# Self attention scores of a decoder layer: products over 64 rows of the array at a time, or over all of it with zero-padded queries and a third key buffer

## The chip, the cores and the metric

One core of one Trainium2 chip runs the whole kernel. The metric is the device time of one execution in microseconds (us). Three executions of the kernel before took 706.29, 706.56 and 707.81 us, so the median is 706.56 us.

## What is computed

The reference is one decoder layer with three sub-layers, each behind a layer norm and added back to its input. `x` is 16 batches of 256 tokens of 128 numbers; the context has 1601 tokens per batch.

```python
xh = x.reshape(b, c, h, he).transpose(0, 2, 1, 3)            # 16 heads of 8
q, k, v = jnp.split(einsum('bhce,ef->bhcf', xh, Wqkv) + bqkv, 3, axis=-1)
att = einsum('bhqe,bhke->bhqk', q, k) / sqrt(8)
att = softmax(att * tril(ones((c, c)), k=-1))                # masked scores count as 0
x = x + (einsum('bhqk,bhke->bhqe', att, v)) @ Wr + br
x = x + cross_attention(layernorm(x), ctx)                   # 1601 keys
x = x + routed_mlp(layernorm(x), top 2 of 8) + shared_mlp(layernorm(x))
```

The change touches only the two products of queries with keys in the self attention.

## The kernel before, in words

**Batches in a pipeline.** Each engine's stream is written out by hand: a `begin()`, a `step(i)` for each batch in the middle, and a `finish()`. In step i the matmul engine (PE) works on the scores of batch i, on the second scores and values of batch i-1, on the output of i-2, on cross attention of i-3 and the gate of i-4. Engines meet by semaphores only, and every engine's list is in order: what waits holds up all behind it.

**Parts.** q and k are split into three bf16 parts each (`split_cast` on ACT, `split_rest` on POOL, L2139 and L2141), so that one bf16 product over 48 rows (6 pairs of parts by 8 elements of a head) has nearly fp32's accuracy. The 16 heads are in two halves, a = 0 and 1, of 8 heads. The tile `parts` goes to DRAM and comes back in another order: `write_parts(b, a)` issues four DMAs on SP's queue (L640 to `q_parts`, three times L642 to `k_stack`), and `load_stack(b, a)` waits until those four have landed, and then issues four loads: keys into `kst` (L655) and three times queries into `qst` (L658). Both tiles have two buffers, for even and odd batches.

**Two scores.** `scores(b, u)`, called for u = 0 to 11, makes two things of each head. For batch b it makes *alpha* (L800), scores with queries on the output's partitions, of which DVE takes the row maxima (L1748, L1752, semaphore `alpha_max`); a last matmul adds the mask (L808, L810). For batch b-1 it makes *gamma* (L803), scores with keys on the partitions and minus the maximum already in them: rows 48 to 50 of the stacks hold the maximum in three bf16 parts and ones. ACT takes the exponential (L1476, `p_exp`), POOL sets the masked part to zero (L2201), and `values` (L840, L843) multiplies by v, in four column strips of 32. Units with u % 3 = 0 hold four heads of 128x128, the others two of 128x256.

**The place in the array.** `rows_of(b, a) = 64 * ((a + b) % 2)`: a batch's half lies in partitions 0 to 47 or 64 to 111, and the half with the same a of the next batch lies in the other one. In a unit, alpha of b and gamma of b-1 therefore use different row halves of the array, and the code issues them in turn.

**Maxima.** At the end of a batch `maxima_T` (L827) transposes the maxima, ACT copies them to `mT` (L1449), and `write_maxima(b)` on SP's queue (L668, two DMAs, one for each half) puts them into rows 48 to 50 of `qst`. `scores(b + 1, 0)` waits for that (`mrows0_in`), for the stack (`stack0_in`), for `alpha_max` and for `p_exp`, all ahead of its first matmul.

**The order on SP's queue**, L640 to L668 among the loads of weights and context:

```python
load_w13(f)                # f = i + 1
write_parts(f, 0)
load_stack(f, 0)
write_maxima(i)
load_info(i - 2, 0), load_infoT(i - 1), load_info(i - 2, 1)     # 1.6 MB of context
write_parts(f, 1)
load_stack(f, 1)
```

Of the kernel before, what the change touches and what calls it, by code (L numbers as in the profile page):

```python
# [16 lines left out]
P = 128  # L17
# [39 lines left out]
QROWS = 48  # L57
KROWS = 51
# [7 lines left out]
def decoder_kernel(nc, x, ctx, ctxT, consts, wq, wk, wv, wr, wx, gate, w13, w2, out):  # L66
    with ExitStack() as stack:
# [3 lines left out]
        def sem(name):  # L71
# [44 lines left out]
        qst = [sb(f"qst{n}", [P, HG, S], BF16) for n in range(2)]  # L116
        kst = [sb(f"kst{n}", [P, HG, S], BF16) for n in range(2)]
# [35 lines left out]
            "split_cast", "split_sub", "parts0_out", "parts1_out", "stack0_in", "stack1_in",  # L153
# [17 lines left out]
        def rows_of(b, a):  # L171

            return 64 * ((a + b) % HA)
# [52 lines left out]
        for n in ("ln3_stats", "ln3_aggr", "ln3_eps", "ln3_rstd", "xn3_done", "xn3T_ps", "xn3T_sb", "x3_hi_done", "x3_lo_done",  # L226
                  "lg_ps", "lg_sb", "route", "shifted", "ex_done", "weigh", "picked", "rank_ps", "rank_read", "row_x", "placed", "sent",
                  "tri_done", "mx_zero", "pad_done", "home_done", "spare_out", "filled_set", "final", "slots_done", "blank_out", "pad_at_done", "info0_in", "info1_in", "x3_copied",
                  "up_ps", "silu_done", "h_done", "y_ps", "shared_done",
                  "in0", "in1", "in2", "in3", "in4", "in5", "sx_ps", "sx_hi", "sx_lo", "sup_ps", "sgate_done", "shid_done", "sT_ps", "sT_sb",  # L230
                  "sy_ps", "sy_sb", "sum_done"):
            s[n] = sem(n)
# [348 lines left out]
        def _(sp):  # L581
# [53 lines left out]
            def write_parts(b, a):  # L635

                if live(b):
                    sp.wait_ge(s["split_sub"], 2 * b + 2)
                    after(sp, f"stack{a}_in", 64 * b)
                    sp.dma_start(dq[a].rearrange("c p t -> p c t"), parts[64 * a:64 * a + 64, :, 0, :]).then_inc(s[f"parts{a}_out"], 16)  # L640
                    for c, (s0, s1) in enumerate(((0, 3), (3, 5), (5, 6))):
                        sp.dma_start(dk[a, s0:s1].rearrange("c p t -> p c t"),  # L642
                                     parts[64 * a:64 * a + 64, c, 1, :].unsqueeze(1).to_broadcast([64, s1 - s0, S])
                                     ).then_inc(s[f"parts{a}_out"], 16)

            def load_stack(b, a):

                if live(b):
                    sp.wait_ge(s[f"parts{a}_out"], 64 * b + 64)
                    if b < 2:  # L650
                        sp.wait_ge(s["pads_done"], 4)
                    else:
                        sp.wait_ge(s["gamma_ps"], 12 * (b - 2) + 6 * a + 6)
                    r = rows_of(b, a)
                    sp.dma_start(kst[b % 2][r:r + QROWS].rearrange("r g t -> r (g t)"),  # L655
                                 dk[a].rearrange("c (e g) t -> (c e) (g t)", e=HE)).then_inc(s[f"stack{a}_in"], 16)
                    for n in (3, 2, 1):
                        sp.dma_start(qst[b % 2][r:r + n * HE].rearrange("r g t -> r (g t)"),  # L658
                                     dq[a, 0:n].rearrange("c (e g) t -> (c e) (g t)", e=HE)).then_inc(s[f"stack{a}_in"], 16)
                        r += n * HE  # L660

            def write_maxima(b):

                if live(b):
                    sp.wait_ge(s["mT_sb"], b + 1)
                    for a in range(HA):
                        q0 = rows_of(b, a) + QROWS
                        sp.dma_start(qst[b % 2][q0:q0 + 3], mT[3 * HG * a:3 * HG * (a + 1)]).then_inc(s[f"mrows{a}_in"], 16)  # L668

            def step(i):  # L670
                f, g, j, k, l = i + 1, i - 1, i - 2, i - 3, i - 4
                load_w13(f)
                write_parts(f, 0)
                load_stack(f, 0)
                write_maxima(i)
                load_info(j, 0)
                load_infoT(g)
                load_info(j, 1)
                write_parts(f, 1)
                load_stack(f, 1)  # L680
                blank_tails(k)
                later_inputs(i)

            def begin():

                load_w13(0)
                later_inputs(-1)
                load_infoT(0)
                load_w13(1)
                write_parts(0, 0)  # L690
                load_stack(0, 0)
# [5 lines left out]
                load_stack(1, 0)  # L697
                write_maxima(0)
                load_stack(1, 1)
# [12 lines left out]
                load_stack(3, 1)  # L712
                later_inputs(2)
# [48 lines left out]
        def _(pe):  # L762
# [12 lines left out]
            def scores(b, u):  # L775
# [4 lines left out]
                if live(b):  # L780
                    if u % 6 == 0:
                        pe.wait_ge(s[f"stack{a}_in"], 64 * b + 64)
                    after(pe, "alpha_max", 12 * b + u - (b < WIDE))
                if live(old):
                    if u % 6 == 0:
                        pe.wait_ge(s[f"mrows{a}_in"], 16 * old + 16)
                        pe.wait_ge(s["alpha_max"], 12 * old + 12)
                    after(pe, "p_exp", 12 * old + u - (old < WIDE - 1 or old == B - 1))
                    if old == B - 1 and u == 1:
                        pe.wait_ge(s["alpha_max"], 12 * B)  # L790
                r, ro = rows_of(b, a), rows_of(old, a)
                q, k = qst[b % 2][r:r + QROWS], kst[b % 2][r:r + QROWS]
                qo, ko = qst[old % 2][ro:ro + KROWS], kst[old % 2][ro:ro + KROWS]
                for c in range(4 if kind == 0 else 2):
                    if kind == 0:
                        h, w, keys, olds, qs = h0 + c, P, slice(0, P), slice(P, S), slice(0, P)
                    else:
                        h, w, keys, olds, qs = h0 + 2 * (kind - 1) + c, S, slice(0, S), slice(0, P), slice(P, S)
                    if live(b):
                        pe.matmul(alpha_bank[:, c * w:(c + 1) * w], lhsT=q[:, h, qs], rhs=k[:, h, keys], start=(c == 0), stop=False,  # L800
                                  skip_group_check=True)
                    if live(old):
                        mm = pe.matmul(gamma_bank[:, c * w:(c + 1) * w], lhsT=ko[:, h, olds], rhs=qo[:, h, olds if kind == 0 else slice(0, S)],  # L803
                                       start=True, stop=True)
                if live(old):
                    mm.then_inc(s["gamma_ps"], 1)
                if live(b):
# [178 lines left out]
            def ranks(i):  # L986
# [9 lines left out]
                if l == 0:  # L996
                    pe.wait_ge(s["tri_done"], 2)
# [300 lines left out]
        def _(act):  # L1298
# [92 lines left out]
            def load_second_stack():  # L1391
                act.wait_ge(s["parts1_out"], 64)
                act.wait_ge(s["pads_done"], 4)
                r = rows_of(0, 1)
                act.dma_start(kst[0][r:r + QROWS].rearrange("r g t -> r (g t)"),
                              dk[1].rearrange("c (e g) t -> (c e) (g t)", e=HE)).then_inc(s["stack1_in"], 16)
                for n in (3, 2, 1):
                    act.dma_start(qst[0][r:r + n * HE].rearrange("r g t -> r (g t)"),
                                  dq[1, 0:n].rearrange("c (e g) t -> (c e) (g t)", e=HE)).then_inc(s["stack1_in"], 16)
                    r += n * HE  # L1400
# [296 lines left out]
        def _(dve):  # L1697
            dve.wait_ge(s["consts_in"], 16)
            dve.tensor_tensor(tri_bf[:], ones, upper, ALU.subtract).then_inc(s["tri_done"], 1)
            dve.tensor_copy(ones_bf[:], ones).then_inc(s["tri_done"], 1)  # L1700
            dve.memset(mx[:], 0.0).then_inc(s["mx_zero"], 1)
            dve.wait_ge(s["mx_zero"], 1)
# [68 lines left out]
            def value_heads(b):  # L1771
                if live(b):
                    dve.wait_ge(s["v_ps"], b + 1)
                    if b < 2:
                        dve.wait_ge(s["pads_done"], 4)
# [663 lines left out]
```

## Time and profile before

| | before |
|---|---|
| median of three executions | 706.56 us |
| span of the profiled execution | 730.5 us |
| PE busy | 651.7 us, 89% of the span |
| DVE, ACT, POOL busy | 59%, 65%, 63% |
| granted PE clock, mean | 0.971 of 2.4 GHz |
| DMA, mean | 107 GB/s |

The profile is one execution, recorded by the hardware profiler; its span from first to last instruction is the only time there is for it, and it is 23.9 us longer than the median of the other executions. Every duration below is from it. "PE busy" counts matmuls from start to end with their way through the array, so that two close matmuls overlap and a pause of less than about 0.2 us between starts doesn't show as idle time; starts are therefore what must be read. In a timeline row the first number is the start, the second the time covered, and "x4" means that four like instructions in a row were merged. "SPq" rows are DMAs that SP's queue issues: the row's time is that of the issue, not of the transfer.

### The profile page before, as it was taken

The page shows a single profiled execution, that of the slowest core. Times are in us where ns is not written, and L with a number is a line of the kernel's source. Part 1 is how long each engine was busy: PE and PEld are TensorE (multiplying, and loading weights), DVE is VectorE, ACT ScalarE, POOL GpSimd, SP SyncE. Part 2 cuts the span into 40 slices and gives each one's busy share as a digit, 9 for nine tenths or more (in the row PEclk, how much of TensorE's full clock was granted, in tenths as well). Part 3 has the DMA queues.
Part 4 walks back from the last instruction along what each step waited for, and adds up shares of the span by engine and source line. Part 5 has one row for each costly group of instructions (what it writes and reads, how often), then busy time and mean ns, then how long its engine had stood idle before and what let it go on. Part 6 is the DMA issues. An engine that isn't in the chain of part 4 may idle for free.

```text
span 730.5 us, 17333 instructions
## 1 busy us (share of the span) xinstructions
PE 651.7 (89%) x5530; PEld 494.9 (68%) x5530; DVE 429.3 (59%) x1168; ACT 472.1 (65%) x1106; POOL 458.5 (63%) x778
## 2 busy tenths in 40 slices
PE   5887899999999999999999999999996798989894
PEld 2344567767677776776867768668785677778674
DVE  2356556867768677686777867746555332322237
ACT  3344687877878878678777886777862354645540
POOL 4345474787877878678786786676655155555560
PEclk9769999999999999999999999999998999999998
DMA  4824526245352453525426245122204232222119
GB/s 137 227 46 123 115 83 188 60 132 147 65 173 48 145 146 78 160 46 147 147 62 171 48 149 146 38 107 92 61 26 108 59 86 81 77 75 68 37 56 309
DMA packets 65111, 77.95 MB, mean 107 GB/s; under 512 B 9314, under 2 KB 50679, under 8 KB 64896
## 3 DMA queue, kind: packets, MB, share of 16 engines
q1 hardware_dynamic: 59884, 67.70, 33.6%
q0 software_dynamic: 4352, 8.47, 3.9%
q8 instruction: 47, 0.77, 0.4%
q10 hardware_dynamic: 788, 0.69, 0.4%
q14 instruction: 40, 0.33, 0.2%
HBM read 54.30 MB, written 22.64 MB: 105 GB/s over the span
## 4 chain that ended last, share of the span: by engine, by line
PE 66%; issue 9%; DVE 6%; ACT 5%; DMA 5%; POOL 4%; SPq 3%; another core or an unknown queue 2%; ACTq 0%; POOLq 0%; DVEq 0%
PE banks L1061 10%; PE banks L1023 7%; PE banks L327 7%; PE banks L800 7%; PE banks L1043 5%; PE banks L349 3%; PE banks L840 3%; PE banks L810 3%; PE banks L808 2%; PE banks L338 2%; PE banks L862 1%; DMA k_stack<-parts 1%; DMA qst<-q_parts 1%; PE banks L843 1%
## 5 line engine op out<-in xcount | busy, mean ns | idle before, releaser
L1476 ACT ACTIVATE prob<-banks 128x512 f32<-128x512 f32 x192 | 114.8, 602 | 63.1 <-PE banks L803 60.7
L2201 POOL TENSOR_SCALAR_AFFINE_SELECT prob<-prob 128x256 f32<-128x256 f32 (+1 forms) x192 | 92.3, 500 | 56.6 <-ACT prob L1476 55.8
L1752 DVE TENSOR_REDUCE mx<-banks 128x2 f32<-128x512 f32 x128 | 87.1, 681 | 42.4 <-PE banks L810 39.2
L1061 PE MATMUL banks<-info,xprobT 128*128 128x128 f32 (+1 forms) x832 | 103.9, 275 | 1.0 <-issue 0.8
L1061 PEld LDWEIGHTS banks<-info,xprobT 128*128 128x128 f32 (+1 forms) x832 | 100.4, 192 | 2.8 <-issue 1.2
L800 PE MATMUL banks<-kst,qst 48*128 48x128 bf16 (+1 forms) x512 | 76.5, 251 | 18.7 <-issue 5.4
L1783 DVE TENSOR_REDUCE xmax<-banks 128x1 f32<-128x896 f32 x64 | 63.0, 985 | 27.7 <-PE banks L1023 18.4
L2226 POOL DMA_INDIRECT sorted_rows<-row,place x64 | 64.4, 1005 | 23.0 <-issue 18.6
L510 DVE TENSOR_TENSOR xprobT<-banks,xprob 128x512 f32<-128x512 f32 x36 | 24.9, 692 | 88.4 <-ACT xprob L419 66.0
L803 PE MATMUL banks<-qst,kst 51*128 51x128 bf16 (+1 forms) x512 | 75.1, 249 | 0.1
L1748 DVE TENSOR_REDUCE mx<-banks 128x4 f32<-128x512 f32 x64 | 44.1, 690 | 45.5 <-PE banks L808 39.1
L1346 ACT COPY xprobT<-banks 128x512 f32<-128x512 f32 (+2 forms) x128 | 64.9, 507 | 8.7 <-PE banks L1043 7.7
L1043 PE MATMUL banks<-cst,xprob 128*128 128x128 f32 (+1 forms) x416 | 68.5, 278 | 1.3 <-issue 0.6
L800 PEld LDWEIGHTS banks<-kst,qst 48*128 48x128 bf16 x512 | 29.3, 95 | 57.0 <-issue 29.7
L1334 ACT ACTIVATE xprob<-banks,xmax 128x896 f32<-128x896 f32 x64 | 59.6, 931 | 3.4 <-DVE xmax L1783 3.1
L536 POOL DMA_INDIRECT routed_out<-vaug,infoT x36 | 35.1, 974 | 38.1 <-ACT vaug L433 29.2
L536 POOL DMA_INDIRECT routed_out<-vaug,info x36 | 35.0, 973 | 30.9 <-ACT vaug L433 22.6
L2190 POOL TENSOR_TENSOR info_lo<-infoT,info_hi 128x896 fp32r<-128x896 f32 (+1 forms) x32 | 53.9, 1686 | 0.0
L1043 PEld LDWEIGHTS banks<-cst,xprob 128*128 128x128 f32 (+1 forms) x416 | 48.1, 145 | 5.5 <-issue 1.9
L1308 ACT ACTIVATE xn<-xall,rstd 128x128 f32<-128x128 f32 x96 | 42.3, 492 | 3.5 <-POOL rstd L2115 3.5
L1023 PE MATMUL banks<-info_hi,q_hi 128*128 128x512 f32 (+1 forms) x96 | 43.1, 449 | 1.6 <-ACT xprob L1334 1.0
L419 ACT ACTIVATE xprob<-banks 128x512 f32<-128x512 f32 x36 | 21.7, 602 | 34.8 <-PE banks L327 29.3
(196 smaller groups left out, 1636.9 us busy)
## 6 DMA issues: line engine op xcount, KB each, us to landing
infoT<-in_ctxT SPq DMA_DIRECT2D x16, 800.5 KB, 5.5
info<-in_ctx SPq DMA_DIRECT2D x16, 448.0 KB, 3.8
kst<-k_stack SPq DMA_DIRECT2D x31, 192.0 KB
info<-in_ctx SPq DMA_DIRECT2D x16, 320.0 KB
q_parts<-parts SPq DMA_DIRECT2D x31, 96.0 KB, 2.3
k_stack<-parts SPq DMA_DIRECT2D x31, 96.0 KB, 2.3
qst<-q_parts SPq DMA_DIRECT2D x31, 96.0 KB
infoT<-sorted_rows SPq DMA_DIRECT2D x36, 65.0 KB
```

What stands on the lines that cost most here:

```text
L536: pool.indirect_dma_start(dy, bass.IndirectOffsetOnAxis(ap=sorted_in[g % SB][:, j % GT, D + 1:D + 2].bitcast(I32), axis=0), routed[j % 8], ...
L800: pe.matmul(alpha_bank[:, c * w:(c + 1) * w], lhsT=q[:, h, qs], rhs=k[:, h, keys], start=(c == 0), stop=False, skip_group_check=True)
L803: mm = pe.matmul(gamma_bank[:, c * w:(c + 1) * w], lhsT=ko[:, h, olds], rhs=qo[:, h, olds if kind == 0 else slice(0, S)], start=True, stop ...
L1023: mm = pe.matmul(ps[:, c, 0:m1 - m0], lhsT=a[:, q], rhs=b[:, m0:m1], start=(n == 0), stop=(n == 2))
L1043: mm = pe.transpose(ps[0:w, XT_BANK, (m - parts_of[z][0]) * P:(m - parts_of[z][0] + 1) * P], xprob[UNITS[u][1]][:, o:o + w], ident)
L1061: mm = pe.matmul(ps[:, V_BANK, u * P:(u + 1) * P], lhsT=xprobT[hf][0:w, m - blocks[0], :], rhs=info[0:w, m, :], start=(m == blocks[0]), st ...
L1346: act.copy(xprobT[hf][:, m0:m1, :], ps[:, XT_BANK, 0:(m1 - m0) * P].rearrange("p (m n) -> p m n", n=P)).then_inc(s["xt_sb"], 1)
L1476: act.activation(prob[n % 2][:, kind * 512:(kind + 1) * 512], ps[:, gamma_bank_of(b, v), :], ACT.Exp, scale=SCALE).then_inc(s["p_exp"], 1)
L1752: dve.tensor_reduce(mx[:, 1, h:h + 2, 0], bank.rearrange("p (c n) -> p c n", c=2), AX.X, ALU.max).then_inc(s["alpha_max"], 1)
L1783: dve.tensor_reduce(xmax[:, u:u + 1], flat(0, HW[UNITS[u][1]]), AX.X, ALU.max, negate=True).then_inc(s["xmax_done"], 1)
L2201: pool.affine_select(out=w, in_=w, compare_op=ALU.is_gt, fill=0.0, base=0, pattern=[[0, 4 if kind == 2 else 2], [1, P]], channel_multiplie ...
L2226: pool.indirect_dma_start(dsort, bass.IndirectOffsetOnAxis(ap=place[:, t, c:c + 1], axis=0), row[:, c, t, :], None, bounds_check=SORTED - ...
```

## The change

Rows 0 to 47 of the stacks are now half 0, rows 48 to 95 half 1, and rows 96 to 101 the maxima (three for each half). `kst` has both halves of the keys under each other, and three buffers. `qst` has all 16 heads side by side, and of a head only the rows of its own half are ever written; the others are set to zero once at the start by DVE. So a product over 96 rows (alpha) or 102 rows (gamma) gives what 48 or 51 gave. In `scores` all gammas of a unit come first, behind the waits for `mrows`, `alpha_max` of the old batch and `p_exp`; then come the waits for keys, queries and the bank of alpha, and all alphas. On SP's queue the keys of both halves are written and loaded ahead of the queries and of `write_maxima`.

```diff
-        qst = [sb(f"qst{n}", [P, HG, S], BF16) for n in range(2)]
-        kst = [sb(f"kst{n}", [P, HG, S], BF16) for n in range(2)]
+        qst = [sb(f"qst{n}", [P, H, S], BF16) for n in range(2)]
+        kst = [sb(f"kst{n}", [P, HG, S], BF16) for n in range(3)]
...
-        def rows_of(b, a):
-
-            return 64 * ((a + b) % HA)
+        def rows_of(a):
+
+            return slice(a * PARTS_ROWS, (a + 1) * PARTS_ROWS)
...
-                    after(sp, f"stack{a}_in", 64 * b)
+                    after(sp, f"q{a}_in", 48 * b)
+                    after(sp, "k_in", 32 * b)
...
-            def load_stack(b, a):
+            def load_k(b, a):
+
+                if live(b):
+                    sp.wait_ge(s[f"parts{a}_out"], 64 * b + 64)
+                    if b < 3:
+                        sp.wait_ge(s["pads_done"], 5)
+                    else:
+                        sp.wait_ge(s["gamma_ps"], 12 * (b - 3) + 12)
+                    sp.dma_start(kst[b % 3][rows_of(a)].rearrange("r g t -> r (g t)"),
+                                 dk[a].rearrange("c (e g) t -> (c e) (g t)", e=HE)).then_inc(s["k_in"], 16)
+
+            def load_q(b, a):
 
                 if live(b):
                     sp.wait_ge(s[f"parts{a}_out"], 64 * b + 64)
                     if b < 2:
-                        sp.wait_ge(s["pads_done"], 4)
+                        sp.wait_ge(s["first_done"], b + 1)
                     else:
                         sp.wait_ge(s["gamma_ps"], 12 * (b - 2) + 6 * a + 6)
...
             def step(i):
                 f, g, j, k, l = i + 1, i - 1, i - 2, i - 3, i - 4
                 load_w13(f)
                 write_parts(f, 0)
-                load_stack(f, 0)
+                load_k(f, 0)
+                write_parts(f, 1)
+                load_k(f, 1)
+                load_q(f, 0)
                 write_maxima(i)
                 load_info(j, 0)
                 load_infoT(g)
                 load_info(j, 1)
-                write_parts(f, 1)
-                load_stack(f, 1)
+                load_q(f, 1)
...
                 write_parts(2, 0)
-                load_stack(2, 0)
+                load_k(2, 0)
+                write_parts(2, 1)
+                load_k(2, 1)
+                load_q(2, 0)
                 write_maxima(1)
-                write_parts(2, 1)
-                load_stack(2, 1)
+                load_q(2, 1)
                 load_infoT(1)
                 write_parts(3, 0)
                 load_info(0, 1)
-                load_stack(3, 0)
+                load_k(3, 0)
+                write_parts(3, 1)
+                load_k(3, 1)
+                load_q(3, 0)
                 write_maxima(2)
-                write_parts(3, 1)
                 load_w13(3)
-                load_stack(3, 1)
+                load_q(3, 1)
...
                 if live(old):
                     if u % 6 == 0:
                         pe.wait_ge(s[f"mrows{a}_in"], 16 * old + 16)
                         pe.wait_ge(s["alpha_max"], 12 * old + 12)
...
                     after(pe, "p_exp", 12 * old + u - (old < WIDE - 1 or old == B - 1))
...
+                    q, k = qst[old % 2][0:GROWS, heads_of(a)], kst[old % 3][0:GROWS]
+                    for c, (h, w, keys, olds, qs) in enumerate(for_heads):
+                        mm = pe.matmul(gamma_bank[:, c * w:(c + 1) * w], lhsT=k[:, h, olds], rhs=q[:, h, olds if kind == 0 else slice(0, S)],
+                                       start=True, stop=True)
+                    mm.then_inc(s["gamma_ps"], 1)
+                if live(b):
+                    if u == 0:
+                        pe.wait_ge(s["k_in"], 32 * b + 32)
+                    if u % 6 == 0:
+                        pe.wait_ge(s[f"q{a}_in"], 48 * b + 48)
+                    after(pe, "alpha_max", 12 * b + u - (b < WIDE))
+                    q, k = qst[b % 2][0:AROWS, heads_of(a)], kst[b % 3][0:AROWS]
+                    for c, (h, w, keys, olds, qs) in enumerate(for_heads):
                         pe.matmul(alpha_bank[:, c * w:(c + 1) * w], lhsT=q[:, h, qs], rhs=k[:, h, keys], start=(c == 0), stop=False,
                                   skip_group_check=True)
...
+            for n in range(2):
+                dve.memset(qst[n][:].rearrange("p g t -> p (g t)").bitcast(F32), 0.0).then_inc(s["first_done"], 1)
             dve.wait_ge(s["consts_in"], 16)
...
             for n in range(2):
                 pool.memset(vaug[n][:], 1.0).then_inc(s["pads_done"], 1)
+            for n in range(3):
                 pool.memset(kst[n][:].rearrange("p g t -> p (g t)").bitcast(F32), TWO_ONES).then_inc(s["pads_done"], 1)
```

Left out are renamed semaphores, the first batch's second half, which ACT's queue loads (its four loads in the same way, keys first), and the changed waits of `vaug`.

## Rows read from the trace of the kernel before

**Rows 1.** The page: its first line, and busy time by engine.
```profile
span 730.5 us, 17333 instructions
PE 651.7 (89%) x5530; PEld 494.9 (68%) x5530; DVE 429.3 (59%) x1168; ACT 472.1 (65%) x1106; POOL 458.5 (63%) x778
```

**Rows 2.** PE's waits, 85.6 to 449.7 us: total us, times, longest.
```profile
PE banks L800 <- issue: 4.7, 15, 0.4
PE banks L800 <- DVE mx L1752: 3.4, 9, 0.5
PE banks L800 <- DMA qst<-q_parts: 2.5, 3, 1.4
PE banks L800 <- ACT prob L1476: 2.1, 9, 0.8
```

**Rows 3.** Timeline of PE, 302 to 304 us, between two units.
```profile
302.04 0.28 PE L800 MATMUL banks<-kst,qst 48*128 48x256 bf16 x1
302.04 0.28 PE L803 MATMUL banks<-qst,kst 51*128 51x256 bf16 x1
...
302.36 0.28 PE L810 MATMUL banks<-mask_bf,ident_bf 128*128 128x256 bf16 x1
...
303.15 0.60 PE L1043 MATMUL banks<-cst,xprob 128*128 128x128 f32 x4
303.68 0.23 PE L800 MATMUL banks<-kst,qst 48*128 48x128 bf16 x1
...
304.01 0.39 PE L808 MATMUL banks<-mask_bf,ident_bf 128*128 128x512 bf16 x1
```

**Rows 4.** Timeline of PE, 199 to 207 us: small matmuls, then the batch's end.
```profile
199.78 0.17 PE L998 MATMUL banks<-oh_bf,tri_bf 128*128 128x16 bf16 x1
199.81 0.17 PE L1000 MATMUL banks<-oh_bf,ones_bf 128*128 128x16 bf16 x1
...
202.88 0.29 PE L827 MATMUL banks<-ident_bf,mq 128*48 128x128 bf16 x2
...
206.05 0.21 PE L800 MATMUL banks<-kst,qst 48*128 48x128 bf16 x1 [0.27 <-issue]
```

**Rows 5.** Timeline of SP's queue, 195 to 214 us, one step.
```profile
195.72 0.58 SPq L640 DMA_DIRECT2D q_parts<-parts  x1
196.34 1.92 SPq L642 DMA_DIRECT2D k_stack<-parts  x3
199.61 0.31 SPq L655 DMA_DIRECT2D kst<-k_stack  x1
199.96 1.14 SPq L658 DMA_DIRECT2D qst<-q_parts  x3
203.60 1.58 SPq L668 DMA_DIRECT2D qst<-mT  x2
...
207.52 0.64 SPq L640 DMA_DIRECT2D q_parts<-parts  x1
...
213.66 0.34 SPq L655 DMA_DIRECT2D kst<-k_stack  x1
```

**Rows 6.** What SP's queue waited for, 85 to 450 us: total us, times, longest.
```profile
SPq L668 <- ACT mT L1449: 28.5, 12, 2.8
```

**Rows 7.** Timeline of POOL, 174 to 206 us: two of its instructions.
```profile
176.69 0.64 POOL L2201 TENSOR_SCALAR_AFFINE_SELECT prob<-prob 128x512 f32<-128x512 f32 x1 [2.36 <-ACT prob L1476]
...
194.53 1.16 POOL L2141 TENSOR_TENSOR parts<-qk_r,parts 128x512 bf16<-128x512 f32 x1
```

**Rows 8.** Timeline of SP's queue, 60 to 64 us, an early step.
```profile
60.59 1.15 SPq L658 DMA_DIRECT2D qst<-q_parts  x3
61.78 1.58 SPq L668 DMA_DIRECT2D qst<-mT  x2
```

**Rows 9.** Timeline of all engines, 0 to 30 us: POOL and DVE after the constants' arrival.
```profile
6.00 0.29 DVE L1699 TENSOR_TENSOR tri_bf<-cst 128x128 bf16<-128x128 f32 x1 [6.00 <-DMA cst<-in_consts]
6.09 0.21 POOL L2097 MEMSET pad<- 128x130 f32 x1 [1.64 <-DMA cst<-in_consts]
```

More of the change, by code:

```diff
@@ L56 @@
 EARLY = 4
-QROWS = 48
-KROWS = 51
+PARTS_ROWS = 48
+AROWS = HA * PARTS_ROWS
+GROWS = AROWS + 3 * HA
 C_ID, C_MASK, C_U, C_ONE, C_CNT, C_BV, C_BR, C_BIAS, C_GB, C_REG, C_SLOT, C_AT, C_TIE, C_K, C_END = 0, 128, 256, 384, 512, 544, 672, 800, 804, 812, 820, 892, 964, 1028, 1044
@@ L169, in live, with heads_of @@
             return 0 <= b < B
-        def rows_of(b, a):
-            return 64 * ((a + b) % HA)
+        def rows_of(a):
+            return slice(a * PARTS_ROWS, (a + 1) * PARTS_ROWS)
+        def heads_of(a):
+            return slice(a * HG, (a + 1) * HG)
         def flat(b0, n):
@@ L650, in load_stack @@
                     if b < 2:
-                        sp.wait_ge(s["pads_done"], 4)
+                        sp.wait_ge(s["first_done"], b + 1)
                     else:
                         sp.wait_ge(s["gamma_ps"], 12 * (b - 2) + 6 * a + 6)
-                    r = rows_of(b, a)
-                    sp.dma_start(kst[b % 2][r:r + QROWS].rearrange("r g t -> r (g t)"),
-                                 dk[a].rearrange("c (e g) t -> (c e) (g t)", e=HE)).then_inc(s[f"stack{a}_in"], 16)
+                    r = a * PARTS_ROWS
                     for n in (3, 2, 1):
-                        sp.dma_start(qst[b % 2][r:r + n * HE].rearrange("r g t -> r (g t)"),
-                                     dq[a, 0:n].rearrange("c (e g) t -> (c e) (g t)", e=HE)).then_inc(s[f"stack{a}_in"], 16)
+                        sp.dma_start(qst[b % 2][r:r + n * HE, heads_of(a)].rearrange("r g t -> r (g t)"),
+                                     dq[a, 0:n].rearrange("c (e g) t -> (c e) (g t)", e=HE)).then_inc(s[f"q{a}_in"], 16)
                         r += n * HE
@@ L690, in begin @@
                 write_parts(0, 0)
-                load_stack(0, 0)
+                load_k(0, 0)
+                load_q(0, 0)
                 load_info(0, 0)
@@ L696, in begin @@
                 write_parts(1, 1)
-                load_stack(1, 0)
+                load_k(1, 0)
+                load_k(1, 1)
+                load_q(1, 0)
                 write_maxima(0)
-                load_stack(1, 1)
+                load_q(1, 1)
                 write_parts(2, 0)
-                load_stack(2, 0)
+                load_k(2, 0)
+                write_parts(2, 1)
+                load_k(2, 1)
+                load_q(2, 0)
                 write_maxima(1)
-                write_parts(2, 1)
-                load_stack(2, 1)
+                load_q(2, 1)
                 load_infoT(1)
@@ L779, in scores @@
                 alpha_bank, gamma_bank = ps[:, bank_of(b, u), :], ps[:, gamma_bank_of(old, u), :]
[L780 to L783, printed above, removed]
+                for_heads = []
+                for c in range(4 if kind == 0 else 2):
+                    if kind == 0:
+                        for_heads.append((h0 + c, P, slice(0, P), slice(P, S), slice(0, P)))
+                    else:
+                        for_heads.append((h0 + 2 * (kind - 1) + c, S, slice(0, S), slice(0, P), slice(P, S)))
                 if live(old):
@@ L787, in scores @@
                         pe.wait_ge(s["alpha_max"], 12 * old + 12)
+                    if old == 0 and u == 0:
+                        pe.wait_ge(s["pads_done"], 5)
                     after(pe, "p_exp", 12 * old + u - (old < WIDE - 1 or old == B - 1))
@@ L790, in scores @@
                         pe.wait_ge(s["alpha_max"], 12 * B)
[L791 to L799, printed above, removed]
+                    q, k = qst[old % 2][0:GROWS, heads_of(a)], kst[old % 3][0:GROWS]
[11 more added lines that the diff above has]
+                    for c, (h, w, keys, olds, qs) in enumerate(for_heads):
                         pe.matmul(alpha_bank[:, c * w:(c + 1) * w], lhsT=q[:, h, qs], rhs=k[:, h, keys], start=(c == 0), stop=False,
                                   skip_group_check=True)
[L802 to L807, printed above, removed]
                     m = (pe.matmul(alpha_bank, lhsT=ident_bf[:], rhs=mask_bf[:].rearrange("p a b -> p (a b)"), start=False, stop=True,
@@ L996, in ranks @@
                 if l == 0:
[L997 removed]
+                    pe.wait_ge(s["first_done"], 4)
                 pe.matmul(ps[:, MISC, 0:2 * E], lhsT=tri_bf[:], rhs=oh_bf[:].rearrange("p t e -> p (t e)"),
@@ L1392, in load_second_stack @@
                 act.wait_ge(s["parts1_out"], 64)
[L1393 to L1396, printed above, removed]
+                act.wait_ge(s["pads_done"], 5)
+                act.dma_start(kst[0][rows_of(1)].rearrange("r g t -> r (g t)"),
+                              dk[1].rearrange("c (e g) t -> (c e) (g t)", e=HE)).then_inc(s["k_in"], 16)
+                act.wait_ge(s["first_done"], 1)
+                r = PARTS_ROWS
                 for n in (3, 2, 1):
-                    act.dma_start(qst[0][r:r + n * HE].rearrange("r g t -> r (g t)"),
-                                  dq[1, 0:n].rearrange("c (e g) t -> (c e) (g t)", e=HE)).then_inc(s["stack1_in"], 16)
+                    act.dma_start(qst[0][r:r + n * HE, heads_of(1)].rearrange("r g t -> r (g t)"),
+                                  dq[1, 0:n].rearrange("c (e g) t -> (c e) (g t)", e=HE)).then_inc(s["q1_in"], 16)
                     r += n * HE
@@ L1697, in _ @@
         def _(dve):
+            for n in range(2):
+                dve.memset(qst[n][:].rearrange("p g t -> p (g t)").bitcast(F32), 0.0).then_inc(s["first_done"], 1)
             dve.wait_ge(s["consts_in"], 16)
[L1699 to L1702, printed above, removed]
+            dve.tensor_tensor(tri_bf[:], ones, upper, ALU.subtract).then_inc(s["first_done"], 1)
+            dve.tensor_copy(ones_bf[:], ones).then_inc(s["first_done"], 1)
+            dve.memset(mx[:], 0.0).then_inc(s["first_done"], 1)
+            dve.wait_ge(s["first_done"], 5)
             dve.tensor_copy(filled[:], cst[:, C_REG:C_REG + E]).then_inc(s["filled_set"], 1)
```

10 lines of the change are left out of this document (5 added, 5 removed).

## The prediction

> **What bounds the kernel now.** I read the page first, then PE's waits, then PE's timeline at two units and at the end of a batch, and then the queue that feeds that end. The page has PE busy for 89% of a span of 730.5 us [rows 1]. In the 364 us of the steady steps PE waits ahead of score matmuls for some 13 us only: 4.7 for "issue", 3.4 for the maxima on DVE, 2.5 for loads of queries, 2.1 for exponentials [rows 2]. So PE's stream is full, and one place of it is fixed from outside: the batch's end. The maxima are transposed at 202.88 us [rows 4], SP's queue writes them at 203.60 [rows 5], and the next batch's first score matmul starts at 206.05, 2.45 us behind that issue, with a small idle mark [rows 4]. That chain has almost no reserve: what comes later there moves the batch. Twelve such batch ends lie in the steady stretch (first scores of batches 4 to 15).
>
> **PE, part by part.** Before, alpha and gamma start together: L800 and L803 both at 302.04 [rows 3]. Two 256-column pairs and the way to the mask matmul take 302.04 to 302.36, 0.32 us; four 128-column pairs take 303.68 to 304.01, 0.33 us. 512 columns at 2.4 GHz are 0.213 us, so about 0.1 us of each is the passage from half-array to full-array matmuls. There is one on the way in too: four fp32 matmuls from 303.15, at 0.11 us each, would let the next start at 303.59, and it starts at 303.68 [rows 3], 0.09 us later. A unit with its entry thus costs 0.41 to 0.42 us of PE's time.
>
> After, a unit is 1024 columns one behind the other, 0.427 us, and with a few nanoseconds more for each matmul, an estimate of mine, 0.437 (four of 256) to 0.447 us (eight of 128). Both passages go, save behind `values` (two units in a step), which leaves other column strips anyway. Without waits: 12 units at +0.02, plus 2 times 0.09 kept, is +0.4 us a step. Waits shift it. Behind a wait for a DMA or an exponential the passage in was hidden, and the unit costs 0.11 more; behind a wait for a maximum the gammas now fill the wait and it costs 0.11 less. Units of both kinds are about equally many (9 and 9 waits, rows 2), so I keep **+0.4 us a step**. Bounds: −0.2 if all waits for maxima turn into work, +1.4 if nothing of the passages goes for half of the units.
>
> Could weight loads for full-array bf16 be the limit instead? L998 and L1000 are full-array bf16 matmuls with different weights and start 0.03 us apart [rows 4], under the 0.053 us of 128 columns, so no. The Trainium skill, "TensorE: Matmul & The Clock Gate", section "Back-to-back issue gap", gives some 81 ns for each 128-column matmul in a stream with weight loads; by that figure a step would cost 1 us more on PE. The row speaks against it. The Trainium skill, "TensorEngine Tiling (Array Packing)", section "Theoretical Speedup", also speaks against this change: small contractions in two row tiles run up to twice as fast; its "Key Properties" says that a change of mode drains the engine, and the 0.09 us above agree. By the first rule alone the scores would lose all that ran side by side, as in the third rival below.
>
> **SP's queue.** Here the change costs time. Before, ahead of `write_maxima(i)` stand only the four writes of half 0 and its four loads. They begin at 195.72, as soon as POOL has made the parts (194.53 + 1.16) [rows 5, 7]; writes to first load take 3.89 us, of which 1.35 is waiting for the landing; the loads end at 201.10, and then the queue waits for the maxima until 203.60, 2.5 us [rows 5]. The sum over the stretch is 28.5 us in 12 waits, **2.4 us** each [rows 6]. After, `write_parts(f, 1)` and `load_k(f, 1)` stand ahead of `write_maxima(i)` too: one more round trip of 3.89 us and one more load of 0.35 us, **4.24 us**, all issued by the queue that has 2.4 us to spare. In the step shown: 195.72 + 3.89 + 0.35 + 3.89 + 0.35 + 1.14 + 0.04 = 205.38 instead of 203.60. The maxima are written 1.8 us late, and with 2.45 us behind it the next batch begins at 207.83 instead of 206.05. Nothing gives this back: PE's first matmul of the batch is a gamma that needs the maxima, and everything of PE is queued behind it. The next parts don't come sooner either. POOL's stretch that ends in them starts with a wait for the batch's own first exponential at 176.69 [rows 7], so it moves with the batch. Sum for 12 batches: 12 × 4.24 − 28.5 = **+22.4 us**.
>
> The same in `begin()`: for batch 2 the maxima are issued at 61.78, directly behind the last load that ends at 61.74 [rows 8], no reserve, so the full 4.2 us count; batch 3 has the same pattern, and there context loads that ran in front of the maxima will be over by then, about −1. Together **+7.4**.
>
> The +0.4 us of PE a step is hidden in the steps whose end the queue sets (1.8 us of idle PE is new there), except what delays POOL's parts. In POOL's list they stand behind `deviation2`, which waits for the output projection, and that stands behind five units on PE, the first of them behind a DMA wait: 0.11 + 4 × 0.017 = +0.17 a step, **+2.0**. In the step of batch 15 there are no parts to write: **+0.4**.
>
> **What gets better.** Half 1's queries were loaded behind 1.6 MB of context and a round trip that took 207.52 to 213.66 there, 6.1 us instead of 3.9 [rows 5]. Now only three loads stand behind the context. The waits for query loads at u = 6 go: **−2.5** [rows 2]. In the twelve units of the last round only gammas run: both passages go and nothing is doubled, 12 × 0.19 = 2.3, part of it beside other waits: **−1.7**.
>
> **At nothing:** DVE's two clearings (it is idle until 6.00 us) and POOL's third `kst` (1.64 us idle ahead of 6.09) [rows 9]; if the constants came sooner they would cost their own few microseconds once. The third key buffer only frees loads earlier, and no load of keys is late. The 96 or 102 rows don't change a matmul's length: with 256 columns one over 48 rows and one over 128 both take 0.28 us [rows 3].
>
> **Sum:** 22.4 + 7.4 + 2.0 + 0.4 − 2.5 − 1.7 = **+28.0 us** on the profiled 730.5 us: 758.5. The runs shown are 3.3% shorter than that execution and nothing says which part of it is shorter. I take +26.5 off the profile's scale (× 0.967 and a little for a queue that may have more reserve), 706.6 + 26.5 = **733 us**. Unknown: if the reserve of the queue is 3 us rather than 2.4 in unprofiled runs, 7 us go; if PE's clock falls in the new pauses (some 5 us long ahead of batches 2 and 3), up to 6 us come.
>
> **Rivals.**
> 1. *The queue has the time after all; PE decides and is even.* If the round trip were hidden (it would have to be under 2.4 + 0.3 us instead of 4.24), what is left is 12 × 0.4 + 0.4 − 2.5 − 1.7 = +1: 707.6 us. For it: nothing but the unprofiled 24 us. Chance 0.05.
> 2. *Faster: gammas fill the waits for maxima.* As rival 1, and the place is the head of each unit: gammas no longer stand behind `alpha_max`, so DVE's reductions run beside them. It decides once the queue's delay is under 0.3 us a step and the waits for maxima (3.4 us, rows 2) and some of the "issue" ones (4.7) turn into work: +1 − 3.4 − 2 = −4.4, 702 us. Against it: the same queue. Chance 0.07.
> 3. *PE loses the doubling and keeps the passages* (the change doesn't do what it is about): the 512 columns that ran beside the others are 0.21 us a unit [rows 3], 2.6 us a step, more than the queue's 1.8, so PE sets the step: 12 × 2.6 + 7.4 = +39, 745 us. Against it: the small matmuls [rows 4]. Chance 0.10.
>
> **How the numbers follow.** Forecast case 0.78: 733, by its own bounds 718 to 742. Range: the upper end 743 leaves out most of rival 3, the lower end 714 takes in more reserve on the queue; rivals 1 and 2 stay outside. A measurement of this kernel can tell about 0.2% (1.4 us) from no change. Faster 0.07, within 0.2% 0.05, slower 0.88.
>
> **What would show it.** In the changed profile: two blocks of L640/L642 writes in a row, each some 3.9 us to the next load, and `write_maxima` directly behind the query loads with no wait for `mT`; PE idle for 1.5 to 2.5 us ahead of the first gamma of each batch, put down to a DMA; batches some 32 us apart instead of 30.3; L803 and L800 starts 0.055 or 0.11 us apart one behind the other, mask matmul 0.44 us after the first; no wait at u = 6. It is wrong if SP's queue still waits for `mT` for over 1 us in most steps, or if PE's idle time ahead of the batches is unchanged.

## The result, and the profile after

The changed kernel takes 752.96 us (four executions, 751.02 to 754.44), the kernel before on the same chip 707.18: the ratio is **1.0625 (1.0577 to 1.0673)**, 45.8 us slower. Forecast were 733 us and a range of 714 to 743. The direction was right, the size was not: +26.5 forecast, +45.8 measured.

First, what the profiles can be compared with. The profile after spans 752.5 us, only 22 more than the 730.5 of the profile before [rows 1]. A second profile of the kernel before (e1 below) and the other runs suggest why. The last part of the program, from the last round's first score matmul to the end, takes 231 or 232 us in every profile from some chips, whatever the version; in every profile from others it takes 251 to 256 us. The profile before has 252 us there and the profile after 231. So the profile before probably came from a chip of the second kind, while the runs of 707 us came from one of the first; its chip isn't on record. A step is one batch: from its first score matmul to that of the next. The steps of the kernel before differ little (30.34 us in the first profile, 30.58 in e1, and 30.34 in e10, which has the same steps on a chip with the short tail). Those of the changed kernel differ more: 33.40 us in the profile after, 34.12 in e5. Below, a step is compared with a step, and a total only with the kernel before on its own chip.

PE's waits in the steady steps of the changed kernel, total us, times, longest (against [rows 2]):

```profile
PE banks L821 <- DMA qst<-mT: 34.1, 13, 4.5
```

The list has two more entries, 0.7 us for "issue" and 0.2 us for ACT, once each. The 10 us of waits for DVE, ACT and "issue" ahead of score matmuls have gone, and one wait stands in their place: the maxima, 34 us. SP's queue in the same stretch (against [rows 6]) no longer waits for the maxima at all (the third entry, left out here, is a load of weights that waits for POOL):

```profile
SPq L646 <- POOL parts L2171: 138.4, 11, 13.3
SPq L660 <- DMA k_stack<-parts: 31.2, 24, 2.0
```

One step of that queue (against [rows 5]; POOL's parts end at 211.58):

```profile
211.61 0.64 SPq L646 DMA_DIRECT2D q_parts<-parts  x1
212.28 1.92 SPq L648 DMA_DIRECT2D k_stack<-parts  x3
215.54 0.33 SPq L660 DMA_DIRECT2D kst<-k_stack  x1
216.00 0.59 SPq L646 DMA_DIRECT2D q_parts<-parts  x1
216.62 1.92 SPq L648 DMA_DIRECT2D k_stack<-parts  x3
219.88 0.31 SPq L660 DMA_DIRECT2D kst<-k_stack  x1
220.28 1.08 SPq L673 DMA_DIRECT2D qst<-q_parts  x3
221.41 1.60 SPq L683 DMA_DIRECT2D qst<-mT  x2
```

Two round trips of 3.9 us stand behind each other, and the maxima are issued at 221.41, directly behind the queries. On PE (against [rows 4]) the batch's end and the next start:

```profile
219.08 0.29 PE L853 MATMUL banks<-ident_bf,mq 128*48 128x128 bf16 x2
...
223.97 0.40 PE L821 MATMUL banks<-qst,kst 102*128 102x128 bf16 x4 [2.00 <-DMA qst<-mT]
```

From the transposed maxima to the next batch are 4.9 us instead of 3.2, and PE idles for 2.0. So far this is the forecast. What it did not have is in the windows behind that pause (columns: length; busy time of PE, its weight loads, DVE, ACT, POOL; granted PE clock; DMA share; GB/s):

```profile
221.90:223.90 2.00, 0.07 (x1) 0.00 (x0) 0.82 (x4) 0.00 (x0) 0.00 (x0) 1.00 0.34 107
223.97:225.25 1.28, 1.27 (x12) 1.06 (x13) 0.27 (x1) 0.84 (x2) 0.17 (x1) 1.00 0.67 165
225.25:228.70 3.45, 3.45 (x16) 2.95 (x15) 2.46 (x10) 0.83 (x2) 2.59 (x7) 0.51 1.00 390
```

Shortly behind the pause the granted clock is 0.51, the lower level of 1.2 GHz, for some 3.4 us, although PE is busy by then. The clock falls so behind nine of the twelve pauses ahead of batches 4 to 15, and nowhere in these steps in the two profiles of the kernel before.

### The profile page after: what moved, and what is told of

It reads as the page before. It is cut to its first block, busy times and chain, and to the rows that moved or that the text cites. A ratio compares the mean times of both kernels' runs of the same rounds, so it can differ in the third digit from the quotient of the medians.

```text
span 752.5 us, 17219 instructions
## 1 busy us (share of the span) xinstructions
PE 662.3 (88%) x5530; PEld 552.3 (73%) x5530; DVE 432.1 (57%) x1170; ACT 472.2 (63%) x1106; POOL 459.1 (61%) x779
## 4 chain that ended last, share of the span: by engine, by line
PE 34%; POOL 20%; DMA 15%; issue 13%; SPq 10%; DVE 6%; ACT 2%; POOLq 0%; ACTq 0%; DVEq 0%
DMA k_stack<-parts 7%; PE banks L332 7%; POOL sorted_rows L2256 5%; SPq L648 4%; PE banks L354 4%; DMA qst<-mT 4%; PE banks L1049 3%; POOL prob L2231 3%; PE banks L1087 3%; PE banks L821 2%; PE banks L832 2%; PE banks L343 2%; SPq L646 2%; DMA sorted_rows<-row,place 2%; POOL info_lo L2220 2%
## 5 line engine op out<-in xcount | busy, mean ns | idle before, releaser
L821 PE MATMUL banks<-qst,kst 102*128 102x128 bf16 (+1 forms) x512 | 76.9, 255 | 39.1 <-DMA qst<-mT 38.1
L832 PE MATMUL banks<-kst,qst 96*128 96x128 bf16 (+1 forms) x512 | 77.9, 256 | 4.4 <-DVE mx L1777 0.9
L821 PEld LDWEIGHTS banks<-qst,kst 102*128 102x128 bf16 x512 | 41.8, 101 | 54.2 <-DMA qst<-mT 41.7
L832 PEld LDWEIGHTS banks<-kst,qst 96*128 96x128 bf16 x512 | 42.2, 102 | 16.3 <-DVE mx L1781 7.4
L1049 PE MATMUL banks<-info_hi,q_hi 128*128 128x512 f32 (+1 forms) x96 | 45.6, 475 | 1.3 <-ACT xprob L1360 1.0
```

Source lines behind the costliest of these rows:

```text
L821: mm = pe.matmul(gamma_bank[:, c * w:(c + 1) * w], lhsT=k[:, h, olds], rhs=q[:, h, olds if kind == 0 else slice(0, S)], start=True, stop=True)
L1049: mm = pe.matmul(ps[:, c, 0:m1 - m0], lhsT=a[:, q], rhs=b[:, m0:m1], start=(n == 0), stop=(n == 2))
```

## The experiments

**e1: the kernel before once more**, to settle which profile to compare with. 

> The kernel before, unchanged, for a second profile. The first profiled execution of it spans 730.5 us where its other executions took 707; up to the first score matmul of the last round it has 478.4 us, and 252 us behind that, while the changed kernel's tail has 231 us. If the 20 us were lost in the tail of that one execution, this profile shows the last round at 478 +- 2 us and a tail of 226 to 232 us, span 704 to 709. If the steps themselves were slower in it, the last round starts at 460 us or less, and the reserve of SP's queue that the prediction used was not that of a usual execution.

Measured: 0.998 (0.994 to 1.002), span 736.4 us. In PE's timeline batch 3 starts at 84.98 and batch 15 at 451.99: 367.0 us for 12 steps, 30.58 each. The last round starts at 480.9, and the tail is 255.5 us again. Neither of the two expected cases came out. On this chip all other executions of the kernel before took about 740 us as well, so a tail of 250 us and more needn't be an accident of one execution, as I had supposed. It goes with the chip: e1 to e4 ran on one, e5 to e8 on a second and e9 to e12 on a third, and the four profiles of a chip agree in the kind of tail. The steps, and with them the reserve of the queue, are alike in both profiles.

**e2: the order of the queue alone.** Row halves and all of PE's code stay as before:

```diff
                 write_parts(f, 0)
-                load_stack(f, 0)
+                load_k(f, 0)
+                write_parts(f, 1)
+                load_k(f, 1)
+                load_q(f, 0)
                 write_maxima(i)
                 load_info(j, 0)
                 load_infoT(g)
                 load_info(j, 1)
-                write_parts(f, 1)
-                load_stack(f, 1)
+                load_q(f, 1)
```

The queue's list for the first batches is changed in the same way.

> Row halves, alternating alpha and gamma, two stacks of keys and all PE code as before; only the order on SP's queue is that of the changed kernel (both halves' writes and keys, then half 0's queries, then the maxima). Theory (the queue's order is the cause): 745 to 755 us, batches 32.5 to 33.5 us apart, PE idle for some 2 us ahead of each batch. Rival (full-array products cost PE the time): 705 to 712 us.

Measured: 794.6 us beside 739.9, ratio **1.074 (1.067 to 1.081)**, steps of 34.6 us. The order by itself costs as much as the whole change; on this kind of chip the changed kernel is at 1.072 (e5). Steps were 1.1 us longer than the most that I had expected; here too the clock falls, behind ten of the twelve pauses.

**e3: the full-array products alone.** Each half gets key columns of its own, so that half 1's keys aren't needed at the batch's start and the order can stay:

```diff
-        kst = [sb(f"kst{n}", [P, HG, S], BF16) for n in range(3)]
+        kst = [k_all[:, n * H * S:(n + 1) * H * S].rearrange("p (g t) -> p g t", t=S) for n in range(2)]
...
-                    q, k = qst[b % 2][0:AROWS, heads_of(a)], kst[b % 3][0:AROWS]
+                    q, k = qst[b % 2][0:AROWS, heads_of(a)], kst[b % 2][0:AROWS, heads_of(a)]
```

> Full-array products over 96 and 102 rows, gammas first, zero-padded queries as in the changed kernel, but each half has key columns of its own (two buffers), so half 1's keys aren't needed at the batch's start, and SP's queue has the order of before. To make room the second expert weights share the key buffers' memory and are loaded after the last gamma. Theory (order is the cause, the products are about even): 703 to 712 us, batches 30 to 31 us apart. Rival (the products cost the time: 2.6 us a step lost on PE): 735 to 750 us.

Measured: **0.997 (0.9935 to 1.0001)**, repeated below at 0.995. Steps of 30.52 us beside 30.58. Neither form of the products loses against the other. A unit at full clock in its timeline:

```profile
283.74 0.39 PE L822 MATMUL banks<-qst,k_all 102*128 102x128 bf16 x4
283.96 0.39 PE L832 MATMUL banks<-k_all,qst 96*128 96x128 bf16 x4
284.19 0.38 PE L834 MATMUL banks<-mask_bf,ident_bf 128*128 128x512 bf16 x1
```

Eight 128-column products, 283.74 to 284.19: 0.45 us, 0.056 us each, and no extra time on the way in or out (the mask matmul of 512 columns takes 0.22 us to the next start, at 284.41). The forecast for the unit was 0.447. Each of the eight has new weights, so their loads run beside the products.

**e4: matmuls in the pause.** Nine 512-column matmuls that compute nothing needed:

```diff
+                    if u == 0 and 1 <= old and live(b):
+                        pe.wait_ge(s["alpha_max"], 12 * old + 12)
+                        pe.wait_ge(s["p_exp"], 12 * old)
+                        for _ in range(9):
+                            pe.matmul(gamma_bank, lhsT=ident_bf[:], rhs=mask_bf[:].rearrange("p a b -> p (a b)"), start=True, stop=True)
```

> The changed kernel with nine more 512-column matmuls (1.9 us) into the free gamma bank ahead of the wait for the maxima of batches 2 to 15, in the pause of 2 to 2.5 us. The granted clock fell to half for 3.4 us behind ten of these pauses. Theory (the fall lengthens the stretch from a batch's start to the parts by 0.7 to 1 us): clock at 1.00 through the steady steps, batches 0.7 to 1 us closer, 738 to 746 us. Rival (the stretch is set by POOL, the clock is beside the point): 750 to 756 us.

**e5: the changed kernel once more**, on a chip of the kind that e1 to e4 ran on. 

> The changed kernel, unchanged, beside the others of this call, since chips differ in the tail (231 us in its first profile, 252 to 256 us in all profiles of the chips used since). Steps 33.3 to 33.6 us, half clock behind most pauses, batch start to parts 20.4 to 20.6 us, ratio 1.055 to 1.065. If the fall of the clock is what lengthens that stretch, the kernel with matmuls in the pause (20.04 us) stays 0.4 us or more below it on a like chip; if not, both show 20.0.

Measured: e5 1.072 (1.059 to 1.085), above the 1.055 to 1.065 that I had expected (the interval is wide because the kernel before ran from 734 to 754 us on that chip); e4 **1.044 (1.036 to 1.052)**. Matmuls that compute nothing needed take off some two fifths of the loss: about 20 us by the ratios, 16 by the spans of the two profiles (786.0 and 770.0), of which 11.6 lie in the twelve steps. (The 738 to 746 us expected for e4 were reckoned from the other kind of chip, 1.044 to 1.055 of the kernel before there; it took 771.8 beside 739.9.) Both kernels behind the start of a batch, columns as above; first e5, with the batch at 228.49:

```profile
229.50:233.00 3.50, 3.50 (x16) 2.87 (x15) 2.33 (x9) 1.09 (x3) 2.76 (x7) 0.51 0.97 377
```

then e4, with the batch at 220.45:

```profile
220.45:224.00 3.55, 3.55 (x31) 3.31 (x32) 2.55 (x9) 2.01 (x4) 2.28 (x6) 1.00 0.90 291
```

31 matmuls start in 3.55 us where in e5 16 start in 3.5. In e5 batch 3 starts at 90.14 and batch 15 at 499.59, 34.12 us a step; e4 has 33.15. Cut at the moment when POOL's parts for the next batch are ready, means over the twelve steps, with e6 and e7 from below:

| | e1, before | e5, changed | e4, matmuls in the pause | e6, both writes first | e7, both |
|---|---|---|---|---|---|
| batch start to parts ready, us | 19.94 | 20.99 | 20.04 | 20.74 | 19.88 |
| parts ready to next start, us | 10.64 | 13.13 | 13.11 | 11.73 | 11.66 |
| step, us | 30.58 | 34.12 | 33.15 | 32.47 | 31.55 |
| falls of the clock behind the 12 pauses | 0 | 9 | 0 | 4 | 0 |

Both parts grew. The second grew by 2.49 us: it is the queue, and e4 leaves it as it is. The first grew by 1.04 us and goes to within 0.10 us of the kernel before when the pause is filled: it is the clock. As e4 and e5 ran on two chips, e6 and e7, both on e5's chip, are the cleaner pair for that, and e6 shows it within one execution.

**e6: both writes first**, then the keys of both halves, the queries and the maxima:

```diff
                 write_parts(f, 0)
-                load_k(f, 0)
                 write_parts(f, 1)
+                load_k(f, 0)
                 load_k(f, 1)
```

> The changed kernel with both halves' writes issued before the first wait for a landing: write half 0, write half 1, keys 0, keys 1, queries 0, maxima. Theory (a step is set by parts, then everything that the queue does ahead of the maxima): one wait for a landing (1.3 us) and what the second write lost behind the 192 KB of keys (0.5 us) go from each of 14 steps: parts to maxima 8.6 to 9.1 us instead of 10.5, ratio 1.025 to 1.035. Rival (only the number of issues counts, or another wait takes its place): ratio above 1.05.

Measured: **1.017 (1.007 to 1.026)**, better than the 1.025 to 1.035 that I had expected; steps of 32.47 us, parts to maxima 9.2 us instead of 10.7. By the medians, moving one load behind one write takes off three quarters of the loss; by the steps of the profiles it takes off about half (34.12 to 32.47, where the kernel before has 30.58), and the profiled execution of e6 was one of its slowest. One wait for a landing is gone from each step, and the clock fell behind four pauses of twelve instead of nine. A step of its queue:

```profile
208.18 0.64 SPq L646 DMA_DIRECT2D q_parts<-parts  x1
208.86 1.93 SPq L648 DMA_DIRECT2D k_stack<-parts  x3
211.25 0.57 SPq L646 DMA_DIRECT2D q_parts<-parts  x1
211.88 1.92 SPq L648 DMA_DIRECT2D k_stack<-parts  x3
213.89 1.53 SPq L660 DMA_DIRECT2D kst<-k_stack  x2
```

This one execution also prices a fall of the clock. Two starts of a batch in it, without a fall (batch 7, at 218.98) and with one (batch 8, at 251.30), columns as above:

```profile
218.98:222.40 3.42, 3.42 (x29) 3.18 (x31) 2.55 (x9) 1.88 (x4) 2.15 (x6) 1.00 0.92 297
251.80:255.20 3.40, 3.40 (x14) 2.80 (x13) 1.37 (x6) 1.01 (x2) 2.57 (x6) 0.50 0.93 350
```

The DMA engines are as busy in both, so their load is not what slows PE here. From the batch's start to the parts the four steps with a fall at their start take 21.69 to 21.75 us. Of the seven without any half clock five take 20.19 to 20.22 and the others 19.50 and 20.75. So 3.4 us at half clock put the parts back by some 1.5 us.

**e7: both writes first, and matmuls in the pause** (six instead of nine). 

> As both writes first, with six 512-column matmuls (1.3 us) into the free gamma bank ahead of the wait for the maxima. If the shorter pause (0.5 to 0.9 us) no longer lets the clock fall, this equals the kernel without them within 0.3%. If the clock still falls there, it is 0.5 to 1.5% faster than it.

Measured: 1.016 (1.007 to 1.026). The profile has no half clock in the twelve steps, and they are 31.55 us instead of 32.47, nearly all of it in the first part (19.88 instead of 20.74). But the profiled execution of e6 was among its slowest (760.4 us; median 754.8) and the medians are 2.8 us apart. So the totals neither show nor exclude a gain here.

**e8: key columns for each half, and at u = 0 the alphas first**, so that they fill the wait for the maxima. 

> Full-array products with key columns for each half and the queue's order of before, and at u = 0 the alphas and the mask ahead of the gammas, so that 0.43 us of PE's work lies in the wait for the maxima. Theory (in that kernel the batch's start is set by the chain maxima, copy, DMA, and PE has some 0.4 us idle in it): 0.3 us less in each of 13 steps, ratio 0.988 to 0.993 against 0.997 without. Rival (POOL or the queue sets the step): 0.995 to 0.998.

**e12: the same again**, beside e11. 

> As e8: with the alphas of u = 0 ahead of the gammas. e8 gave 0.992 (0.988 to 0.996), but its steps in the trace were like e3's (30.47 and 30.52 us), so that the trace shows no gain from the alphas' place. If that is right this equals e11 within 0.3%; if the gain is real it is 0.3 to 0.7% below e11.

**e11: e3 again.** 

> As e3: full-array products, gammas first, the queue's order of before. In e3 0.997 (0.9935 to 1.0001), in steps 0.06 us apart from the kernel before. Expected 0.994 to 1.000.

**e10: only the later load of the second expert weights**, which e3, e8, e11 and e12 have too. 

> The kernel before, in which only the second expert weights (1.15 MB) are loaded after the last gamma instead of at batch 2, as in the kernels with key columns for each half. If that load explains their gain, this is at 0.99 to 0.997. If not, at 0.998 to 1.002.

Measured: e8 0.992 (0.988 to 0.996); then, on one chip beside the same runs of before, e10 0.998 (0.9945 to 1.002), e11 **0.995 (0.991 to 0.998)**, e12 0.9955 (0.993 to 0.9985). So the full-array products with key columns of their own and the later load together beat the kernel before by about half a per cent (706.9 us beside 709.7). What part of it the products have isn't shown: the later load alone took 708.6, and the intervals overlap. The alphas' place at u = 0 gives nothing: e8's better number was not repeated, and its steps had said so (30.47 us, e3 30.52). I had expected 0.3 us a step from it; what sets that kernel's step is not PE's work at this place.

**e9: the changed kernel with the maxima issued from ACT's queue**, and no longer from SP's:

```diff
                     act.copy(mT[:], ps[0:3 * H, MISC, 0:S]).then_inc(s["mT_sb"], 1)
+                    act.wait_ge(s["mT_sb"], b + 1)
+                    for a in range(HA):
+                        q0 = AROWS + 3 * a
+                        act.dma_start(qst[b % 2][q0:q0 + 3, heads_of(a)], mT[3 * HG * a:3 * HG * (a + 1)]).then_inc(s[f"mrows{a}_in"], 16)
```

> The changed kernel with the two maxima DMAs issued from ACT's queue, directly behind ACT's own copy of them, so that SP's queue no longer stands between. Theory (everything that the queue does behind the parts sets the step, the maxima are only its last piece): the gammas start as early as before (parts + 10.7 us), but then the alphas wait for half 0's queries, whose last load is issued near parts + 10.4 us: the wait moves from L821 to L832 (queries), a step is 0.5 to 1 us shorter than the changed kernel's 34.1, ratio 1.05 to 1.065. Rival (the position of the maxima alone is the cause): ratio 1.00 to 1.01.

Measured: **1.050 (1.0445 to 1.056)** on the chip where before takes 710. PE's waits in its steady steps:

```profile
PE banks L828 <- issue: 14.9, 12, 3.2
PE banks L1083 <- ACT xprobT L1368: 13.5, 12, 1.1
```

The wait for the maxima has gone from the gammas (L817), and two others stand there. One is 15 us ahead of the alphas (L828): the profile puts it down to nothing, and that line's wait at u = 0 is for keys and queries, so that the queue holds them is argued and not shown. The other is 13.5 us for ACT's copies, which now stand behind ACT's own DMA issues (at 219.19 ACT issues the maxima for 1.47 us, and its next copy, which PE waits for, starts at 220.71). That is a cost of the experiment, some 1.1 us of the 2.4 by which its steps (32.73 us) exceed those of e10 on the same chip. So moving the maxima alone doesn't bring back the time of before, and 15 us still stand ahead of the alphas; how much would be left with a free queue for the maxima isn't shown.

## Why the prediction was partly right

**Right.** The bound (the batch's start hangs on SP's queue, not on PE's work): e2 and e3 separate the two cleanly, 1.074 for the order and 0.997 for the products. That PE comes out about even: forecast +0.4 us a step before waits, and unit times of 0.437 to 0.447 us, measured 0.45. Rival 3 (2.6 us a step lost on PE) falls with e3. The Trainium skill, "TensorE: Matmul & The Clock Gate", section "Back-to-back issue gap", gives some 81 ns for a 128-column matmul in a stream with weight loads; here it is 0.056 us, and the measurement decides. Rivals 1 and 2 fall with the queue's waits. The waits at u = 6 have gone, as forecast.

**Right by luck.** Batches 2 and 3 together were forecast 7.4 us longer; e5 has 49.6 us for them (23.4 + 26.2) where e1 has 42.1, +7.5. But the parts of that sum don't fit: batch 2 was given 4.2 us and took 2.2, batch 3 was given 3.2 and took 5.3. And batch 1 starts 2.4 us earlier than in e1 (40.50 and 42.88), which was not forecast, so that batch 3 starts only 5.2 us later.

**Wrong: the sum of the twelve steady steps.** Forecast was 22.4 (queue) + 2.0 − 2.5 = 21.9 us. On chips with the long tail (e5 against e1) they are 42.4 us longer; the first two profiles give 36.7. Two terms failed.

1. *The step "batch start to parts moves with the batch", taken at +2.0 − 2.5.* Measured 12 × 1.04 = 12.5 us (10.1 in the first two profiles). The fall of PE's clock stood outside the sum: it was named for the new pauses, sized by those of some 5 us ahead of batches 2 and 3, as "up to 6 us". It comes behind pauses of 1.9 us and more in e5, nine of twelve, and e4 shows that 0.95 us of the 1.04 go when the pause is filled; nine falls at the 1.5 us of e6 are 13. The kernel before gave no row for that: its longest idle time of PE in these steps was 1.4 us, without a fall. The term should have had an upper bound from the stretch at 33 to 50 us of the same profile, where the granted clock is 0.50: some microseconds at half clock in each of 12 steps is what a range to 743 had no room for.
2. *The size of the second round trip, 4.24 us less 2.4 of reserve.* The second writes were taken at the price of the first, and the first at the price of one step. The queue's extra time turned out as 2.49 us a step, not 1.87: 12 × 0.62 = 7.4 us (4.1 in the first two profiles). The 3.89 us from the first write to the first load are those of the step shown; the mean over the twelve steps of the same profile is 4.07. In e5 the first trip takes 4.17 us and the second 4.45, and with the load between them the second adds 4.88 where the forecast had 4.24. The second takes 3.9 us in four of the twelve steps and 4.5 to 5.5 in the others. It runs behind the keys' load of 192 KB; whether that is the reason is not shown.

Together 12.5 + 0.5 + 7.4 = 20.4 us, and the difference between 42.4 and 21.9 is 20.5.

The rest: the last step was +1.2 us, forecast +0.4. The gain of 1.7 us in the last round doesn't show: from its first to its last gamma it takes 17.9 us in the profile after and 17.6 in e10, whose products are those of before, both on chips with the short tail. Scaling the sum by 0.967 because the runs were shorter than the profile was wrong in its reason: some 20 of the 24 us lay in that profile's long tail, and the steps needed no scaling. It took 1.5 us off the forecast.

## What to carry to other kernels

Before something is put ahead of a DMA that an engine's next stretch hangs on, add up the whole queue from the event that starts it, with every wait for a landing as a term of its own, and compare with the queue's wait at that place: here 4.2 us were put into 2.4. Issue all writes before the first wait for one. And price a new pause of PE twice: once as the pause, and once as what runs at half clock behind it (here 1.5 us a fall, behind most of the pauses of 2 to 3 us).

## What I had not expected of the hardware

- The granted clock fell to 0.5 for 3.4 us, at times 6.8, behind nine of the twelve pauses of e5, four times when PE was busy again (at 229.53 for a batch that starts at 228.49) and five times still in the pause (at 191.98 for one that starts at 194.11). The length of the pause alone doesn't decide: there was no fall behind 2.95 us in e5, and one behind 1.45 us in the profile after. In e4, with the same queue but pauses of at most 1.7 us, it fell behind none of the twelve.
- The kernel before isn't safe from it either: in e10, which differs from it only by the later load of weights, the clock fell twice for 6.8 us in the middle of a batch, behind idle times of PE of 1.96 and 1.71 us.
- The passage between half-array and full-array matmuls costs some 0.09 us each way (302.16 to 302.36 us in rows 3 for a 256-column product, where 256 columns at 2.4 GHz are 0.107). Two of them, 0.19 us, are about what running two halves side by side wins for products of this size, 0.21 us. e3, which gives up both, is even.
- Two kinds of chip differ by 20 to 25 us in the last 230 to 256 us of this program, behind the first 90 us of that stretch. Why stays open.
